# First attention's key roots: four GpSimd powers replaced by eleven VectorE instructions

## The chip, the cores and the metric

The kernel runs on one core of one Trainium2 chip. The metric is the device time of one execution in microseconds (us). One profiled execution gives the trace from which every row below is read; times of single instructions are in that trace's us, counted from the start of its span.

## The reference, cut to what matters

Four sublayers are applied to x of shape 16 x 256 x 128, each between two layer norms with a residual: a phasor convolution, a mixture of 8 experts, a 16-head attention with l2-normed queries and keys, and a second mixture. The part that the change touches is the norm of the keys:

```python
def _l2norm(t):
    return t / jnp.maximum(jnp.linalg.norm(t, axis=-1, keepdims=True), 1e-12)
q = _l2norm(q) * q_scale
k = _l2norm(k) * k_scale
sim = jnp.einsum('bhid,bhjd->bhij', q, k) * ATTN_SCALE
...
attn = jax.nn.softmax(sim, axis=-1)
```

One reciprocal root per token and head is needed for the keys, 128 x 64 numbers for a group of 512 tokens.

## The kernel before, in words

The 16 sequences go through in G = 8 groups of two. A group is 512 tokens, T = 4 tiles of 128, with tokens on the partitions. Up to four groups are under way at once, each in another sublayer. Each engine plays a list of steps in an order written out by hand: `PROLOGUE`, `FIRST`, `MIDDLE` (five times), `LAST_L`, `LAST_A`, `LAST_F`. A name like `a_kss.0.1` is a step and its arguments. In `FIRST` the attention (`a_`) of group 0 runs beside the first mixture (`l_`) of group 1 and the convolution (`e_` for group 2, `E_` for group 1). Engines meet only through semaphores, and each engine takes its list in order, so a step that waits holds up all that stand behind it.

The steps around the change, in group 0:

- ScalarE squares the keys, and TensorE sums the squares by head (`a_kr`) and turns the sums (`a_kt`). VectorE's `a_kss` (`a_ksums`, L1579) clamps the sums and divides by 64, 128x64 in `k_sumsq`.
- GpSimd's `a_kss.b.part` (`k_norms`, L943) raises them to -0.5, in four instructions of 128x16 numbers each, into `rnorm[:, 0]`. In `FIRST` GpSimd's list has them as "a_ss.2 a_kss.0.0 l_turn2 a_ss.3 l_res a_kss.0.1 a_keep a_kss.1.0 a_kss.1.1 e_stats a_scores.0". Here `a_ss.t` (L937) is the same power for the queries of tile t, and `l_turn2`, `l_res`, `e_stats` (L894) are the roots of the layer norms n_y, n_l, n_x.
- ScalarE's `a_scores.c` (L1198 to L1207) takes the exponents of one pair of score tiles with `rnorm[:, 0]` as the scale. It waits for the semaphore `a_kroot`, which counts four in all: step c needs c // 2 + 1. GpSimd's `a_scores.c` then masks (L951) and adds (`late_sum`, L961, which writes the tile mixed), and TensorE's `a_mix.c` uses the mask (L2075) and the sum (L2078).
- VectorE's list in `FIRST` reads "a_kss a_u.2 l_turn2 a_ss.3 l_res a_u.3 l_norm e_stats a_nexp l_turn3 l_route l_pick l_coef l_hg.0 l_hu.0 e_apply l_hg.1". `a_u.t` (L1587) scales the queries of a tile by their roots; `l_turn2` (L1388 to L1393) and `l_res` (L1398 on) are layer norm work, `e_apply` (L1398 too, xn from xin) waits for GpSimd's `e_stats`, and `l_hg.1` (L1528) frees the bank that TensorE's `l_g.2` (L1770) writes. `e_scan` (L1450) is a scan of the convolution.
- TensorE's list has "l_route l_g.0 a_scores.0 l_u.0 l_cT a_nT l_g.1 l_u.1 a_scores.1 l_g.2 a_mix.0 l_c.0 a_scores.2 a_mix.1". The scores are L2028 and L2034; tanh of `l_g.j` on ScalarE is L1127.

Of the kernel before, what the change touches and what calls it, by code (L numbers as in the profile page):

```python
# [20 lines left out]
I32 = mybir.dt.int32  # L21
U32 = mybir.dt.uint32
ALU = mybir.AluOpType
# [52 lines left out]
a_scores.5 a_scores.6 a_scores.7 l_x.0 l_x.1  # L76
""",
    "POOL": """
E_stats a_ss.0 a_ss.1 E_scan a_ss.2 a_kss.0.0 l_turn2 a_ss.3 l_res a_kss.0.1 a_keep a_kss.1.0 a_kss.1.1 e_stats
a_scores.0 a_scores.1 a_scores.2 a_scores.3 e_scan a_scores.4 a_scores.5 a_scores.6 l_dstats.0 a_scores.7 l_dstats.1  # L80
l_astats.0 l_astats.1 a_o.0 a_o.1
""",
# [147 lines left out]
def program(nc, a, out):  # L230
# [4 lines left out]
    T = SEQ * L // P  # L235
    N = T * P
    H, DH, NULLS = 16, 64, 2
# [16 lines left out]
    with ExitStack() as ctx:  # L254
        def sb(name, shape, dt=F32):
            return ctx.enter_context(nc.sbuf_tensor(name, shape, dt))

        def sem(name):
            return ctx.enter_context(nc.semaphore(name))

        def signal(name, per):
            return Signal(sem(name), per)
# [99 lines left out]
        rnorm = sb("rnorm", [P, 2, T, 16])  # L362
# [33 lines left out]
        k_square = [unit[:, i // 2, i % 2, :] for i in range(4)]  # L396
# [168 lines left out]
        a_ss = signal("a_ss", 2 * T)  # L565
# [3 lines left out]
        a_kturn = signal("a_kturn", 1)  # L569
        a_kss = signal("a_kss", 1)  # L570
        a_kroot = signal("a_kroot", 4)
        a_unit = signal("a_unit", T)
        a_s = signal("a_s", H)
        a_odd1 = signal("a_odd1", H // 2)
# [146 lines left out]
        def known(g):  # L721
            return isinstance(g, int)

        def first(g):
            return known(g) and g == 0
# [532 lines left out]
        def _(dve):  # L1258
# [12 lines left out]
            V = nc.vector  # L1271
# [303 lines left out]
            def a_ksums(g):  # L1575
                dve.wait_ge(a_kturn.sem, a_kturn.at(g))
                if not first(g):
                    dve.wait_ge(a_kroot.sem, a_kroot.at(g - 1))
                V.tensor_scalar(k_sumsq.rearrange("p t (c j) -> p t c j", j=4),  # L1579
                                bank[3][:].rearrange("p (t c j) -> p t c j", t=T, j=32)[:, :, :, 0:4],  # L1580
                                1e-24, 1.0 / 64.0, ALU.max, ALU.mult).then_inc(a_kss.sem, 1)

            def a_units(g, t):
                dve.wait_ge(a_root.sem, a_root.at(g, t + 1))
                dve.wait_ge(a_took.sem, a_took.at(g, use("m", t, 1) + 1))
                raw = unit[:, t % 2, 2:4, :].rearrange("p j (h d) -> p (j h) d", d=DH)
                V.tensor_tensor(raw, raw, rnorm[:, 1, t, :].unsqueeze(2).to_broadcast([P, H, DH]), ALU.mult).then_inc(a_unit.sem, 1)  # L1587
# [157 lines left out]
            def f_end(g):  # L1745
# [8 lines left out]
                "l_norm": l_norm, "l_turn3": l_turn3, "l_ct": l_cT, "l_xl": l_xl, "l_route": l_route, "l_pick": l_pick_, "l_coef": l_coef, "l_hg": l_hg_, "l_hu": l_hu_,  # L1754
                "l_hc": l_hc_, "l_dstats": l_down_, "l_end": l_end, "l_astats": a_stats, "l_aapply": a_apply,
                "a_null": a_null, "a_ss": a_sums, "a_kss": a_ksums, "a_u": a_units,
                "a_nexp": a_nexp_, "a_nt": a_nrows_, "a_mix": a_mixes, "a_o": a_out_, "a_end": a_end,
                "f_stats": f_stats, "f_apply": f_apply, "f_turn": f_lows, "f_route": f_route, "f_pick": f_pick_, "f_ce": f_ce_,
# [471 lines left out]
def build(nc, inputs):  # L2230

    arrays, args = {}, {}
    for name, value in inputs.items():
        v = np.ascontiguousarray(value)
        arrays[f"in_{name}"] = v
        args[name] = nc.dram_tensor(f"in_{name}", v.shape, mybir.dt.from_np(v.dtype), kind="ExternalInput").ap()
    out = nc.dram_tensor("out_0", inputs["L0_attn_x"].shape, F32, kind="ExternalOutput").ap()
    program(nc, args, out)
    return arrays
# [10 lines left out]
```

## Time and profile before

| | |
|---|---|
| median of 3 runs | 931.28 us (929.42 to 932.6) |
| the profiled execution's own time | 930.28 us |
| its span | 928.6 us |
| busy share | PE 94%, PEld 75%, DVE 83%, ACT 63%, POOL 61% |
| granted clock of TensorE, mean | 0.997 |

The span is what the trace covers; the execution's own time is 1.68 us more, for what lies around it. PE is TensorE's matmuls, PEld its weight loads, DVE VectorE, ACT ScalarE, POOL GpSimd. A busy share is a mean over the whole span, and says nothing of the one stretch in which the first attention runs.

### The profile page before, as it was taken

How to read it: one execution, taken by the hardware profiler on the slowest of the kernel's cores; microseconds unless marked ns; L12 is line 12 of the kernel's file. 1: busy time of each engine (PE TensorE's matmuls, PEld its weight loads, DVE VectorE, ACT ScalarE, POOL GpSimd, SP SyncE). 2: the span in 40 equal slices, each digit the busy share in tenths (PEclk: the TensorE clock that was granted, in tenths of full speed). 3: DMA queues.
4: the chain of work that ended last, by engine and by line, in shares of the span. 5: the costliest groups of instructions: out<-in, count | busy, mean ns of one | idle time of the engine just before them, and what ended most of it. 6: DMA issues, size and time to landing. Idle time of an engine off the chain costs nothing.

```text
span 928.6 us, 21350 instructions
## 1 busy us (share of the span) xinstructions
PE 874.9 (94%) x8095; PEld 692.8 (75%) x8095; DVE 767.0 (83%) x2457; ACT 586.4 (63%) x1255; POOL 568.4 (61%) x503
## 2 busy tenths in 40 slices
PE   0997899999999999999999999999999999998886
PEld 0675678687877878687777878688787878777666
DVE  6787898789998899889997899879997678865576
ACT  4528773876477672976557672976648683885631
POOL 5118773687557774677547874668635964487623
PEclk9999999999999999999999999999999999999999
DMA  6400000000000000000000000000000000000000
GB/s 161 117 1 0 13 2 1 1 13 1 14 1 1 12 2 13 1 13 2 13 2 1 12 2 14 1 12 2 14 1 1 2 1 14 0 1 1 14 1 12
DMA packets 21991, 11.46 MB, mean 12 GB/s; under 512 B 7552, under 2 KB 21248, under 8 KB 21760
## 3 DMA queue, kind: packets, MB, share of 16 engines
q1 hardware_dynamic: 20032, 9.50, 3.7%
q8 instruction: 64, 1.05, 0.5%
q10 hardware_dynamic: 1856, 0.59, 0.3%
q14 instruction: 39, 0.32, 0.1%
HBM read 7.99 MB, written 2.10 MB: 11 GB/s over the span
## 4 chain that ended last, share of the span: by engine, by line
PE 75%; DVE 8%; POOL 8%; ACT 5%; issue 3%; DMA 0%; DVEq 0%; POOLq 0%; ACTq 0%
PE bank L1770 8%; PE bank L1772 7%; PE bank L1771 7%; PE bank L2100 6%; PE bank L1783 5%; PE bank L1936 4%; PE bank L2028 4%; PE bank L2085 4%; PE bank L2202 3%; PE bank L2208 3%; PE bank L2034 3%; PE bank L2087 2%; PE bank L1992 2%; POOL mixed L961 2%; PE bank L2177 2%
## 5 line engine op out<-in xcount | busy, mean ns | idle before, releaser
L937 POOL TENSOR_TENSOR rnorm<-sumsq,minus_half 128x16 f32<-128x16 f32 x32 | 95.8, 2994 | 57.3 <-DVE sumsq L1573 57.2
L1201 ACT ACTIVATE square<-bank,bias_k,rnorm 128x256 f32<-128x256 f32 x128 | 65.8, 571 | 54.0 <-PE bank L2028 54.0
L2028 PE MATMUL bank<-qT,kT 64*128 64x256 f32 x512 | 96.6, 387 | 0.0
L943 POOL TENSOR_TENSOR rnorm<-unit,minus_half 128x16 f32<-128x16 f32 x32 | 93.3, 2928 | 1.6 <-DVE unit L1579 1.6
L2034 PE MATMUL bank<-qT,kT 64*128 64x128 f32 x512 | 84.0, 284 | 5.5 <-ACT unit L1207 3.9
L2034 PEld LDWEIGHTS bank<-qT,kT 64*128 64x128 f32 x512 | 71.0, 186 | 18.8 <-ACT unit L1207 6.1
L951 POOL TENSOR_SCALAR_AFFINE_SELECT square<-square 128x512 f32<-128x512 f32 x64 | 45.2, 707 | 48.9 <-ACT square L1207 48.7
L1131 ACT ACTIVATE xaT_hi<-bank 128x256 fp32r<-128x256 f32 x16 | 5.9, 384 | 108.5 <-PE bank L1944 108.2
L2028 PEld LDWEIGHTS bank<-qT,kT 64*128 64x128 f32 x512 | 68.8, 186 | 0.2
L951 POOL TENSOR_SCALAR_AFFINE_SELECT unit<-unit 128x512 f32<-128x512 f32 x64 | 41.0, 646 | 40.6 <-ACT unit L1207 40.6
L2100 PE MATMUL bank<-w_out,qT 128*128 128x128 f32 x512 | 62.7, 276 | 1.5 <-DVE qT L1622 1.5
L2100 PEld LDWEIGHTS bank<-w_out,qT 128*128 128x128 f32 x512 | 59.7, 192 | 2.1 <-DVE qT L1622 1.7
L1201 ACT ACTIVATE unit<-bank,bias_k,rnorm 128x256 f32<-128x256 f32 x96 | 51.4, 574 | 15.3 <-PE bank L2028 15.3
L1587 DVE TENSOR_TENSOR unit<-unit,rnorm 128x1024 f32<-128x1024 f32 x32 | 45.7, 1427 | 15.1 <-POOL rnorm L937 15.1
L1207 ACT ACTIVATE unit<-bank,bias_k,rnorm 128x128 f32<-128x128 f32 x128 | 52.7, 478 | 0.0
L1207 ACT ACTIVATE square<-bank,bias_k,rnorm 128x128 f32<-128x128 f32 x128 | 52.4, 473 | 0.0
L1570 DVE TENSOR_REDUCE sumsq<-square 128x16 f32<-128x1024 f32 x32 | 38.9, 1215 | 13.2 <-ACT square L1147 13.2
L1783 PEld LDWEIGHTS bank<-ident,unit 128*128 128x128 f32 x296 | 33.7, 141 | 20.1 <-DVE unit L1587 10.5
L1167 ACT ACTIVATE qT<-bank,qk_scale 128x512 f32<-128x512 f32 x64 | 40.5, 689 | 11.5 <-PE bank L1783 11.5
L1140 ACT ACTIVATE unit<-bank 128x512 f32<-128x512 f32 x64 | 36.8, 600 | 16.0 <-PE bank L1772 15.0
L1622 DVE TENSOR_TENSOR qT<-bank,mixed 128x512 f32<-128x512 f32 x64 | 44.2, 691 | 2.2
L1783 PE MATMUL bank<-ident,unit 128*128 128x128 f32 x296 | 39.7, 275 | 6.6 <-DVE unit L1587 3.6
(419 smaller groups left out, 2910.3 us busy)
## 6 DMA issues: line engine op xcount, KB each, us to landing
xin<-in_L_attn_x SPq DMA_DIRECT2D x7, 256.0 KB, 2.8
out<-x SPq DMA_DIRECT2D x7, 256.0 KB, 2.3
square<-in_L_attn_w_kv SPq DMA_DIRECT2D x1, 1024.0 KB, 6.3
unit<-in_L_attn_w_q SPq DMA_DIRECT2D x1, 512.0 KB, 5.6
w_out<-in_L_attn_w_out SPq DMA_DIRECT2D x8, 64.0 KB, 2.1
xin<-in_L_attn_x ACTq DMA_DIRECT2D x1, 256.0 KB, 3.1
unit<-in_L_ffn_experts_gate ACTq DMA_DIRECT2D x1, 256.0 KB, 3.4
unit<-in_L_ffn_experts_up SPq DMA_DIRECT2D x1, 256.0 KB, 2.9
```

The lines of the kernel that those rows point to most:

```text
L937: pool.tensor_tensor(rnorm[:, 1, t, :], sumsq[:, t % 2, :], minus_half[:], ALU.pow).then_inc(a_root.sem, 1)
L943: pool.tensor_tensor(rnorm[:, 0, ts, hs], k_sumsq[:, ts, hs], minus_half[:, hs].unsqueeze(1).to_broadcast([P, 2, H // 2]), ALU.pow).then_i ...
L951: pool.affine_select(out=pd, in_=pd, compare_op=ALU.is_ge, fill=0.0, base=0, pattern=[[0, 4], [1, P]], channel_multiplier=-1).then_inc(a_m ...
L1201: last = act.activation(early(pr, j), k0, ACT.Exp, bias=bias_k0[:, h:h + 1], scale=by)
L1207: last = act.activation(late(pr, j), bank[2][:, 2 * P * s + P * j:2 * P * s + P * (j + 1)], ACT.Exp, bias=bias_k1[:, h:h + 1], scale=by)
L1770: mm(dst, left.hi, right.hi, start=True, stop=False)
L1771: mm(dst, left.hi, right.lo, start=False, stop=False)
L1772: return mm(dst, left.lo, right.hi, start=False, stop=True)
L1783: last = nc.tensor.transpose(dst[:, t * P:(t + 1) * P], src(t), ident[:])
L2028: return mm(bank[s][:, 2 * P * i:2 * P * (i + 1)], kT[rs, p, 2 * P * b:2 * P * b + P], qT[rs, p, 2 * P * b:2 * P * (b + 1)], start=True, s ...
L2034: return mm(bank[2][:, 2 * P * s + P * i:2 * P * s + P * (i + 1)], kT[rs, p, ts], qT[rs, p, ts], start=True, stop=True)
L2100: mm(out_bank(g, h)[:, ts], outT[:, c, ts], w_out[:, c, :], start=(c == 0), stop=False)
```

## The change

The four `a_kss` steps are gone from GpSimd's list in `FIRST`; the lists of the other stages keep theirs. VectorE, right behind the clamp of `a_kss` and only in group 0, runs a new function `k_roots`. It shifts the bits of the number right by one, takes them from a constant, and improves the guess by three Newton steps of three instructions: 11 instructions over 128x64 numbers, each waiting for the one before it through the new semaphore `k_newton`. The last raises `a_kroot` by four.

```diff
-E_stats a_ss.0 a_ss.1 E_scan a_ss.2 a_kss.0.0 l_turn2 a_ss.3 l_res a_kss.0.1 a_keep a_kss.1.0 a_kss.1.1 e_stats
+E_stats a_ss.0 a_ss.1 E_scan a_ss.2 l_turn2 a_ss.3 l_res a_keep e_stats
...
+        k_newton = sem("k_newton")
...
                                 1e-24, 1.0 / 64.0, ALU.max, ALU.mult).then_inc(a_kss.sem, 1)
+                if first(g):
+                    k_roots()
+
+            def k_roots():
+
+                ss = k_square[1][:, 0:T * H]
+                tmp = k_square[1][:, T * H:2 * T * H]
+                y = rnorm[:, 0, :, :].rearrange("p t h -> p (t h)")
+                dve.wait_ge(a_kss.sem, a_kss.at(0))
+                V.tensor_scalar(tmp.bitcast(I32), ss.bitcast(I32), 1, None, ALU.logical_shift_right).then_inc(k_newton, 1)
+                dve.wait_ge(k_newton, 1)
+                V.tensor_scalar(y.bitcast(I32), tmp.bitcast(I32), -1.0, float(0x5f3759df), ALU.mult, ALU.add).then_inc(k_newton, 1)
+                for k in range(3):
+                    dve.wait_ge(k_newton, 3 * k + 2)
+                    V.scalar_tensor_tensor(out=tmp, in0=y, scalar=-0.5, in1=y, op0=ALU.mult, op1=ALU.mult).then_inc(k_newton, 1)
+                    dve.wait_ge(k_newton, 3 * k + 3)
+                    V.tensor_tensor(tmp, tmp, ss, ALU.mult).then_inc(k_newton, 1)
+                    dve.wait_ge(k_newton, 3 * k + 4)
+                    done = V.scalar_tensor_tensor(out=y, in0=tmp, scalar=1.5, in1=y, op0=ALU.add, op1=ALU.mult)
+                    if k < 2:
+                        done.then_inc(k_newton, 1)
+                    else:
+                        done.then_inc(a_kroot.sem, 4)
```

## Rows read from the trace of the kernel before

**Rows 1.** The page: busy time, share of the span and instructions of each engine.
```profile
PE 874.9 (94%) x8095; PEld 692.8 (75%) x8095; DVE 767.0 (83%) x2457; ACT 586.4 (63%) x1255; POOL 568.4 (61%) x503
```

**Rows 2.** Busy time of each engine in two stretches (us; count in brackets).
```profile
85.00:110.00 25.00, 18.61 (x118) 14.45 (x116) 19.88 (x75) 19.73 (x44) 22.68 (x13) 1.00 0.04 11
110.00:135.00 25.00, 24.84 (x356) 18.30 (x355) 23.97 (x48) 18.03 (x44) 15.72 (x17) 1.00 0.01 3
```

**Rows 3.** The chain that ended last: start us, us, what.
```profile
99.54 5.72 POOL rnorm L943 x2
```

**Rows 4.** Timeline of POOL: start us, us, what [idle before <-releaser].
```profile
85.56 3.81 POOL L943 TENSOR_TENSOR rnorm<-unit,minus_half 128x16 f32<-128x16 f32 x1 [1.61 <-DVE unit L1579]
89.34 1.00 POOL L894 TENSOR_TENSOR n_y_rstd<-n_y_var,minus_half 128x4 f32<-128x4 f32 x1
90.32 2.89 POOL L937 TENSOR_TENSOR rnorm<-sumsq,minus_half 128x16 f32<-128x16 f32 x1
94.08 1.92 POOL L894 TENSOR_TENSOR n_l_rstd<-n_l_var,minus_half 128x4 f32<-128x4 f32 x1 [0.87 <-DVE n_l_var L1393]
...
106.20 1.22 POOL L951 TENSOR_SCALAR_AFFINE_SELECT unit<-unit 128x512 f32<-128x512 f32 x2
...
111.91 1.27 POOL L961 TENSOR_TENSOR mixed<-square 128x512 f32<-128x512 f32 x1
...
118.11 1.27 POOL L961 TENSOR_TENSOR mixed<-unit 128x512 f32<-128x512 f32 x1
```

**Rows 5.** Timeline of DVE, 85 to 106 us.
```profile
85.26 0.23 DVE L1579 TENSOR_SCALAR unit<-bank 128x64 f32<-128x64 f32 x1 [2.71 <-PE bank L1783]
85.40 1.22 DVE L1587 TENSOR_TENSOR unit<-unit,rnorm 128x1024 f32<-128x1024 f32 x1
87.09 0.89 DVE L1388 BATCH_NORM_STATS2 n_y_six<-bank 128x6 f32<-128x128 f32 x4 [0.48 <-PE bank L1783]
...
88.51 1.22 DVE L1570 TENSOR_REDUCE sumsq<-square 128x16 f32<-128x1024 f32 x1
89.77 0.18 DVE L1573 TENSOR_SCALAR sumsq<-sumsq 128x16 f32<-128x16 f32 x1
90.38 1.37 DVE L1398 TENSOR_SCALAR xn<-bank,n_y_mv,n_y_rstd 128x128 f32<-128x128 f32 x4 [0.44 <-POOL n_y_rstd L894]
```

**Rows 6.** Timeline of DVE, 106 to 122 us.
```profile
106.27 2.84 DVE L1398 TENSOR_SCALAR xn<-xin,n_x_mv,n_x_rstd 128x128 f32<-128x128 f32 x4 [1.15 <-POOL n_x_rstd L894]
...
111.95 0.17 DVE L1613 TENSOR_TENSOR den<-bank,null_sum 128x8 f32<-128x8 f32 x1
112.15 0.20 DVE L1617 RECIPROCAL recip<-den 128x8 f32<-128x8 f32 x1
...
118.48 3.10 DVE L1450 TENSOR_TENSOR_SCAN conv<-decay_row,conv 128x512 f32<-128x512 f32 x2
```

**Rows 7.** Single lines of DVE: count, duration in ns min/median/max, first and last start.
```profile
L1627 DVE TENSOR_TENSOR mixed<-mixed,recip x16: 214/215/651, 127.3 to 884.8; 128x64 f32<-128x64 f32 x16
L1593 DVE SCALAR_TENSOR_TENSOR null_s<-null_s,bias_null x8: 291/1128/1133, 98.8 to 829.3; 128x128 f32<-128x128 f32 x8
L1398 DVE TENSOR_SCALAR xn<-x,n_l_mv,n_l_rstd x4: 343/344/346, 96.0 to 96.8; 128x128 f32<-128x128 f32 x4
```

**Rows 8.** Timeline of PE.
```profile
91.16 0.63 PE L1783 MATMUL bank<-ident,unit 128*128 128x128 f32 x4 [2.28 <-ACT val L1174]
...
106.62 0.37 PE L2034 MATMUL bank<-qT,kT 64*128 64x128 f32 x1 [0.35 <-ACT unit L1207]
...
109.77 0.50 PE L1770 MATMUL bank<-xlT_hi,w_gate_hi 128*128 128x512 f32 x1 [1.57 <-DVE unit L1528]
...
112.55 0.60 PE L2034 MATMUL bank<-qT,kT 64*128 64x128 f32 x3
...
114.52 0.40 PE L2078 MATMUL bank<-mixed,ones 128*32 128x128 f32 x8
```

**Rows 9.** Timeline of ACT.
```profile
110.29 0.83 ACT L1207 ACTIVATE square<-bank,bias_k,rnorm 128x128 f32<-128x128 f32 x2
```

## The prediction

> **What bounds the kernel now.** I read the page first. TensorE is busy for 94% of the span [rows 1], so in most places only a change of its work or of its few waits moves the end. The stretches say that the first attention is one of the other places: from 85 to 110 us TensorE works 18.61 of 25 us, and GpSimd, with 22.68, is the busiest engine; from 110 to 135 us TensorE works 24.84 of 25 again and VectorE 23.97 [rows 2]. So whatever the change brings has to be read from the first stretch, and what counts is how much earlier or later TensorE comes out of it.
>
> The chain in order of time seems to settle the matter: it runs through GpSimd's key roots, 5.72 us of them at 99.54 [rows 3], right up to the root of n_x for which `e_apply` waits. GpSimd's timeline gives the four pieces as 3.81 at 85.56, one of some 2.9 behind the root of n_l (94.08 to 96.00), and 5.72 [rows 3, 4]. But the chain goes back along an engine that is always busy. The waits are what other engines pay for it, and they are small: VectorE waits 0.44 us for the root of n_y before `l_res` (90.38), and 1.15 us for n_x before `e_apply` (106.27) [rows 5, 6]. TensorE's own wait is 1.57 us at `l_g.2`, for VectorE's `l_hg.1`, which stands right behind `e_apply` [rows 8]. That is the place where GpSimd's lateness reaches TensorE.
>
> **What is removed.** Four powers go, 3.81 + 2.9 + 5.72 = 12.4 us of GpSimd. The scores' exponents don't wait for them (the first piece is there at 89.4, and ScalarE reaches `a_scores.0` only behind 100 us). What comes sooner is what stood behind: the root of n_y, which could start when VectorE has its variance (about 88.7, not 89.34), and the root of n_x, ready some 4 us before VectorE gets to `e_apply`. VectorE's steps before `e_apply` end at about 105.1, so it would save the 1.15 us of waiting, and `e_apply` itself, 2.84 us beside GpSimd's masks, where four tensor_scalars of this shape at 0.34 us each take 1.4 at most [rows 6, 7].
>
> **What is added.** Eleven instructions over 128x64 numbers on VectorE, each waiting for the last. No row shows the two on integers, nor such a chain. The nearest in width is L1627, two SBUF inputs, 128x64, 0.215 us at the median; a tensor_scalar of 128x64 from PSUM takes 0.23 [rows 7, 5]. The gap to the next one that waits for it: a 0.17 us instruction at 111.95 is followed at 112.15, so 0.03 to 0.04 [rows 6]. I take 0.215 + 0.04 = 0.255 a step, p, and 11 p = 2.8 us. Bounds: from below the narrowest dependent one, 0.17 + 0.04 = 0.21, giving 2.3; from above a tensor_scalar twice as wide, 0.343 + 0.04 = 0.38, giving 4.2 [rows 7].
>
> A rule speaks here, and against many small instructions. The 11 steps cost nearly as much as wide ones would: 8 numbers a partition take 0.17 us, 64 take 0.215 [rows 6, 7]. The Trainium skill (VectorE: DVE Perf Modes, section on the TRN2 errata) says that an SBUF instruction pays a fixed extra cost, with a table entry of 58 cycles plus the width at 0.96 GHz. By that table a step would be 0.13 us, 11 of them 1.4 us without gaps, and the change would come to 1.4 - 2.4 = -1.0 us by the sum below; the same section says that the table is too low for single instructions, and the rows agree with that.
>
> **What stands behind the Newton steps.** `a_u.2`, `l_turn2`, `a_ss.3`, `l_res`, in order. The clamp starts at 85.26 and ends at 85.49; the next one that waits for it starts at 85.53. The chain ends at 85.53 + 2.8 = 88.3. Independent instructions start 0.09 before the end of the last (85.40 against 85.49), so `a_u.2` starts at 88.2 instead of 85.40. Before, VectorE then had 0.48 us of waiting for TensorE (87.09) and the 0.44 us above; now both are gone and all is back to back. By the starts in rows 5: `a_u.2` 1.22 - 0.09 = 1.13; the statistics of `l_turn2` 88.51 - 87.09 = 1.42; the sum of `a_ss.3` 89.77 - 88.51 = 1.26; its clamp 0.18 - 0.09 = 0.09; together 3.90. `l_res` starts at 88.2 + 3.9 = 92.1 instead of 90.38. I call this delay S: S = 11 p - 1.1 = 1.7 us. GpSimd is idle by then; the root of n_y is out 3.8 us behind the start of `a_u.2`, just in time, and is not the last to come.
>
> What of the work between is hidden: TensorE's `a_t.2` needs `a_u.2`, now at 89.5 rather than 88.3, but its second half waits until 91.16 for ScalarE to free a bank anyway [rows 8]. From `l_res` on VectorE, TensorE and ScalarE wait for one another (root of n_l, `l_turn3`, `l_route`, the scores), with no slack that I can find, so all of it comes S later up to `a_scores.1` on TensorE at 106.62 + 1.7.
>
> **What is given back.** Behind `a_scores.1`, TensorE had 1.57 us of waiting at 109.77 [rows 8]. `e_apply` no longer waits and is over long before ScalarE's tanh, so `l_hg.1` comes in time and `l_g.2` starts S - 1.57 = 0.15 us later than before. The pair of scores that ScalarE takes next ends at 111.12 + S (110.29 + 0.83) [rows 9], and frees a bank for `a_scores.2`, which started at 112.55: it has 1.37 us of slack [rows 8], 0.06 less the hand-over. GpSimd's add of that pair ends at 113.18 + S (111.91 + 1.27) [rows 4], and TensorE's `a_mix.1` wanted it at 114.52, so with 0.05 for the hand-over there were 1.29 us of slack [rows 8]. The last one binds: TensorE goes on S - 1.3 = 0.4 us later. Behind it TensorE is full [rows 2], and nothing later is tied to a fixed time, so 0.4 us stay to the end.
>
> In one line: change = 11 p - 1.1 - 1.3 = 11 p - 2.4. If the Newton steps cost nothing, `l_turn2` would still wait for TensorE until 87.09 and S would be -0.5, the change -1.8 us: this is all that GpSimd's 12.4 us are worth. With p = 0.21 it is -0.1, with 0.255 +0.4, with 0.38 +1.8. On the profiled execution's 930.28 us the likeliest is 930.7. The median of the runs shown is 1.0 above that execution; on it, 931.28 + 0.4 = 931.7. Its own range is 931.2 to 933.1, before the scatter of the runs, which is 3.2 us wide over three. A difference under 0.3%, 2.8 us, is about what a measurement of this kernel can't tell from none.
>
> **The rivals.**
>
> The chain is right (5%). If GpSimd's pieces lay on the path in full, 12.4 - 2.8 = 9.6 us would go: 921.7. For it speaks only the chain [rows 3]; against it the waits of 0.44 and 1.15 us, and that the pair of 5.72 us holds back nothing but the root of n_x and the masks.
>
> The Newton steps are dear (8%). Each is a wait on VectorE's own semaphore, and two of them are on integers. L1593, a two-input instruction like six of these, takes 1.13 us at the median where it falls beside GpSimd's powers, and 0.29 where it doesn't [rows 7]. GpSimd is idle from 84 to 91 us in the new order, so I don't expect it. From p = 0.47 on the change is over +2.8 us, and at 0.6 it is +4.2: 935.5.
>
> The engines collide elsewhere (12%). `e_apply` took 2.84 us beside masks from 106.20, and the two scans 3.10 us at 118.48 beside an add at 118.11 to 119.38 [rows 4, 6]. In the new order the first is at about 106.8 to 108, beside only one mask. Should the add and the scan part as well, up to 1.27 us of blocking comes back, and the change is 0.4 - 1.3 = -0.9: 930.4. Should they collide anew, it is +1.7: 933. Both are within 0.3%. The Trainium skill (SBUF — State Buffer, section Who interferes with whom) has it that a VectorE instruction with two SBUF inputs and a GpSimd one that reads SBUF exclude each other, and that the second to issue stands until the first is done. The trace agrees where it can be seen: 2.84 against 1.4 us.
>
> The change does nothing measurable for other reasons, my sum being off by a slack that I missed on either side: that is inside the forecast.
>
> **How the numbers follow.** My sum (within 0.3%) has 75%, the collisions 12%, both no difference; the chain 5%, dear steps 8%. The rest of the doubt is the scatter, which can push either side over the bound. Faster by over 0.3%: 0.09; within: 0.81; slower: 0.10. The range goes from the collisions' gain less scatter, 929.0, to the upper bound of p (933.1) with scatter, 934.2; outside stay the chain and dear steps, and a little scatter.
>
> **What would show it.** In the new profile: GpSimd idle from 84 to some 91 us; eleven instructions of 128x64 from 85.5 to 88.3 on VectorE; `a_u.2` at 88.2; `l_res` at 92.1 with no wait for the root of n_y; `a_scores.1` on TensorE at 108.3; no wait of TensorE for L1528 at `l_g.2`, which starts at about 109.9; `e_apply` with no wait and under 2 us; TensorE's L2078 of `a_mix.1` at 114.9. I am wrong if the steps take more than 0.38 us each, if something between 92 and 106 us had slack that takes S up, or if a stretch behind 115 us gives back or adds more than a microsecond.

## The result, and the profile after

| | before | changed |
|---|---|---|
| median | 930.07 us (20 runs, 929.42 to 932.72) | 932.60 us (20 runs, 932.17 to 934.20) |
| profiled execution's own time | 930.28 us | 932.91 us |
| span | 928.6 us | 931.2 us |

The ratio is 1.0027, interval 1.0021 to 1.0034: the changed kernel is 2.5 us slower. That is just inside the 0.3% that I called no difference, and with twenty runs of each it is a difference all the same. I forecast +0.4 us.

Timeline of VectorE in the changed kernel, 85 to 109 us (start us, us, line, operation). These are the rows that answer to [rows 5]:

```profile
85.55 0.23 DVE L1580 TENSOR_SCALAR unit<-bank 128x64 f32<-128x64 f32 x1 [2.70 <-PE bank L1807]
85.81 0.20 DVE L1592 TENSOR_SCALAR unit<-unit 128x64 int32<-128x64 int32 x1
86.04 0.20 DVE L1594 TENSOR_SCALAR rnorm<-unit 128x64 int32<-128x64 int32 x1
86.27 0.23 DVE L1597 SCALAR_TENSOR_TENSOR unit<-rnorm 128x64 f32<-128x64 f32 x1
...
88.42 0.23 DVE L1601 SCALAR_TENSOR_TENSOR rnorm<-unit,rnorm 128x64 f32<-128x64 f32 x1
88.56 1.22 DVE L1611 TENSOR_TENSOR unit<-unit,rnorm 128x1024 f32<-128x1024 f32 x1
...
92.45 1.36 DVE L1399 TENSOR_SCALAR xn<-bank,n_y_mv,n_y_rstd 128x128 f32<-128x128 f32 x4
...
98.09 1.38 DVE L1399 TENSOR_SCALAR xn<-x,n_l_mv,n_l_rstd 128x128 f32<-128x128 f32 x4 [0.90 <-POOL n_l_rstd L895]
...
102.49 0.69 DVE L1477 TENSOR_TENSOR xlT_lo<-bank,xlT_hi 128x512 fp32r<-128x512 f32 x1 [1.10 <-ACT xlT_hi L1112]
...
108.54 1.24 DVE L1399 TENSOR_SCALAR xn<-xin,n_x_mv,n_x_rstd 128x128 f32<-128x128 f32 x4
```

This execution is 0.29 us later than the one before already at 34 us and again at 84.6 us, ahead of the change, so that much has to be taken off. The eleven steps then take 85.81 to 88.65, 2.84 us; `l_res` starts at 92.45 and no longer waits for a root; `e_apply` (108.54) doesn't wait either and is down from 2.84 to 1.24 us. But at 102.49 VectorE waits for ScalarE, which it didn't before. TensorE, which was to be S later and no more, shows why. The eight transposes of `a_t.3` before:

```profile
95.19 1.09 PE L1783 MATMUL bank<-ident,unit 128*128 128x128 f32 x8 [1.98 <-DVE unit L1587]
```

TensorE's timeline in the changed kernel:

```profile
91.46 0.63 PE L1807 MATMUL bank<-ident,unit 128*128 128x128 f32 x4 [0.96 <-ACT val L1175]
...
97.25 1.82 PE L1807 MATMUL bank<-ident,unit 128*128 128x128 f32 x8 [3.74 <-DVE unit L1611]
98.72 0.78 PE L1794 MATMUL bank<-w_kv_hi,xaT_hi 128*128 128x512 f32 x1
99.29 0.63 PE L1795 MATMUL bank<-w_kv_lo,xaT_hi 128*128 128x512 f32 x1
...
101.84 0.39 PE L1795 MATMUL bank<-w_kv_lo,xaT_hi 128*128 128x512 f32 x1
```

And the busy time by stretch (PE, PEld, DVE, ACT, POOL, then the granted clock):

```profile
85.00:97.00 12.00, 6.46 (x34) 4.70 (x33) 10.76 (x39) 7.70 (x15) 4.77 (x3) 1.00 0.07 22
97.00:101.00 4.00, 3.75 (x14) 3.33 (x15) 3.03 (x15) 1.97 (x3) 1.67 (x3) 0.57 0.02 4
101.00:105.00 4.00, 3.93 (x23) 2.85 (x21) 1.65 (x9) 2.28 (x4) 0.96 (x1) 1.00 0.00 0
```

TensorE stood idle for 3.74 us ahead of `a_t.3`, where it had waited 1.98 us before. From 97.4 us its granted clock is half, 1.2 of 2.4 GHz, for 3.4 us. The same matmul takes 0.63 us at 99.29 and 0.39 us at 101.84, and eight transposes take 1.82 us where they took 1.09.

To see where each run gains or loses, I took the start of the n-th matmul of TensorE less that of the same matmul in the kernel before, at points named by their time there. The last column but one is the stage by itself: the shift at 140 us less that at 84.6.

| run | 84.6 | 95.2 | 101.5 | 109.8 | 119 | 140 | stage | end |
|---|---|---|---|---|---|---|---|---|
| changed | +0.29 | +2.06 | +3.51 | +1.87 | +2.27 | +2.17 | +1.87 | +2.63 |
| x1_warm | +0.16 | +1.94 | +2.20 | +0.56 | +0.96 | +0.86 | +0.69 | +1.30 |
| x2_two_steps | +0.45 | +1.44 | +2.71 | +1.07 | +1.46 | +1.35 | +0.89 | +1.79 |
| x3_order | -0.06 | -0.05 | +1.63 | -0.01 | +0.39 | +0.32 | +0.38 | +0.32 |
| x4_add_only | +1.92 | +3.62 | +4.95 | +3.31 | +3.70 | +3.60 | +1.68 | +3.61 |
| x5_fill | +1.32 | +3.09 | +3.36 | +1.71 | +2.10 | +1.98 | +0.66 | +2.17 |
| x6_behind | -0.09 | -0.63 | +1.52 | -0.13 | +0.27 | +0.21 | +0.30 | +0.63 |
| x7_split | +0.38 | -0.15 | +0.37 | -1.09 | -0.72 | -0.82 | -1.21 | -0.88 |
| x8_one_step | +0.47 | +0.68 | +0.93 | -0.71 | -0.31 | -0.41 | -0.88 | +0.04 |
| x9_split_keep | -0.16 | -0.70 | -0.57 | -1.74 | -1.34 | -1.45 | -1.29 | -1.33 |
| x10_split_fill | -0.38 | -0.92 | -0.79 | -1.97 | -1.58 | -1.66 | -1.28 | -1.81 |
| x11_before_fill | -0.30 | -0.30 | -0.30 | -0.30 | -0.29 | -0.28 | +0.02 | -0.31 |
| x12_seed | +0.17 | -0.37 | -0.10 | -1.74 | -1.34 | -1.45 | -1.63 | -1.42 |

In the changed kernel S is 2.06 - 0.29 = 1.77 us at `a_t.3`; it jumps by 1.45 up to 101.5, and 1.64 comes back at `l_g.2`. The first column differs from run to run, ahead of any difference between the kernels, so a single execution can't be compared at its end; the stage column can. What the first column follows is the clock: matmuls of 128x512 that take 0.63 us at first take 0.39 us from about 31.9 us on in the kernel before, from 32.6 in the changed kernel (+0.29) and from 33.1 in x8 (+0.47), and in x4 and x5 (+1.92, +1.32) the clock was at half once more from 50.8 to 54.2 us.

### The profile page after: what moved, and what is told of

Its sections match the earlier page's. It is cut to its first block, busy times and chain, and to the rows that moved or that the text cites. A ratio compares the mean times of both kernels' runs of the same rounds, so it can differ in the third digit from the quotient of the medians.

```text
span 931.2 us, 21358 instructions
## 1 busy us (share of the span) xinstructions
PE 877.2 (94%) x8095; PEld 694.1 (75%) x8095; DVE 765.5 (82%) x2468; ACT 586.8 (63%) x1255; POOL 556.9 (60%) x499
## 4 chain that ended last, share of the span: by engine, by line
PE 74%; DVE 9%; POOL 7%; ACT 6%; issue 3%; DMA 0%; DVEq 0%; ACTq 0%; POOLq 0%
PE bank L1794 8%; PE bank L1796 7%; PE bank L1795 7%; PE bank L2124 6%; PE bank L1807 5%; PE bank L1960 4%; PE bank L2052 4%; PE bank L2109 4%; PE bank L2226 3%; PE bank L2232 3%; PE bank L2058 3%; POOL mixed L962 2%; PE bank L2111 2%; PE bank L2016 2%; PE bank L2201 2%
## 5 line engine op out<-in xcount | busy, mean ns | idle before, releaser
L944 POOL TENSOR_TENSOR rnorm<-unit,minus_half 128x16 f32<-128x16 f32 x28 | 81.0, 2905 | 0.0
```

What stands on the lines that cost most here:

```text
L944: pool.tensor_tensor(rnorm[:, 0, ts, hs], k_sumsq[:, ts, hs], minus_half[:, hs].unsqueeze(1).to_broadcast([P, 2, H // 2]), ALU.pow).then_i ...
```

## The experiments

Two theories. **Cold clock:** the delay by itself is worth what my sum says, and the rest is TensorE's pause, which lowers its clock. **Missed slack:** each us that VectorE is late reaches the end, and the clock has no part in it.

**x1_warm.** Dummy matmuls ahead of `a_t.3`:

```diff
             def a_t(g, t):
+                if first(g) and t == 3:
+                    for _ in range(8):
+                        mm(bank[4][:], w_kv.hi[:, 0:P], w_kv.hi[:, 0:N], start=True, stop=True)
```

> The changed kernel with eight matmuls of 128x512 (1.9 us) whose result nothing reads, on TensorE right ahead of a_t.3, where it stands idle for 3.74 us in the changed kernel. The cold-clock theory (the pause lowers the granted clock to 0.5 for 3.4 us, and this costs some 1.5 of the 2.5 us): no stretch of lowered clock between 90 and 105 us, time 1.5 us under the changed kernel, +1.0 us against the kernel before (ratio about 1.001). The missed-slack theory (every us that VectorE is later reaches the end, whatever the clock): time as the changed kernel, +2.5 us (1.0027).

Measured: median 933.20 us (6 runs), ratio 1.0030 (1.0018 to 1.0042). By the median, no help. But the profiled execution, at 931.58 the fastest of the six, is the one with the clock up. Its TensorE and its stretches:

```profile
97.13 1.09 PE L1807 MATMUL bank<-ident,unit 128*128 128x128 f32 x8 [1.92 <-DVE unit L1611]
97.98 0.48 PE L1794 MATMUL bank<-w_kv_hi,xaT_hi 128*128 128x512 f32 x1
```

```profile
97.00:101.00 4.00, 3.87 (x23) 3.29 (x24) 3.00 (x16) 3.04 (x6) 1.67 (x3) 1.00 0.00 0
```

The stage costs 0.69 us here and 1.87 us in the changed kernel, with the same delay at `a_t.3` (1.78 and 1.77): the clock is 1.2 us. The other five runs, at 933.03 to 933.85, had a mean clock of 0.992 to 0.994 against 0.996. They have no trace, so that the clock fell in this stage there is likely and not shown. x5 fills all three pauses.

**x2_two_steps.** `for k in range(2)` in `k_roots`, the roots less exact.

> The changed kernel with two Newton steps instead of three: 8 instructions instead of 11, the roots less exact. VectorE is 0.78 us earlier, and TensorE's pause ahead of a_t.3 is 2.96 us instead of 3.74. The cold-clock theory: if the clock stays up over the shorter pause, 0.8 + 1.5 = 2.3 us under the changed kernel, +0.2 us against the kernel before (1.000); if it falls all the same, +1.7 us (1.0018). The missed-slack theory: +1.7 us with the clock at 1.00.

Measured: median 931.93 us, ratio 1.0017 (1.0008 to 1.0026). TensorE's pause was 2.98 us, and the clock fell:

```profile
96.63 1.09 PE L1807 MATMUL bank<-ident,unit 128*128 128x128 f32 x8 [2.98 <-DVE unit L1611]
```

```profile
97.70:101.00 3.30, 3.30 (x12) 2.62 (x11) 2.97 (x15) 2.09 (x4) 0.97 (x2) 0.50 0.00 0
```

The stage is 0.98 us under the changed kernel's, of which 0.78 are three instructions of 0.26. The time fits both theories; only the clock, which missed slack wants at 1.00, is against that one: it was 0.50.

**x3_order.** The kernel before, with GpSimd's list changed and a wait that keeps `l_hg.1` from overwriting the sums:

```diff
-... l_res a_kss.0.1 a_keep a_kss.1.0 a_kss.1.1 e_stats
+... l_res a_kss.0.1 a_keep e_stats a_kss.1.0 a_kss.1.1
...
                 dve.wait_ge(l_tanh.sem, l_tanh.at(g, j + 1))
+                if known(g) and g == 1 and j == 1:
+                    dve.wait_ge(a_kroot.sem, a_kroot.at(0))
```

> The kernel before (roots on GpSimd) with e_stats moved up in GpSimd's list, ahead of the last two key pieces, and l_hg.1 waiting for these. My sum says that GpSimd's pieces cost TensorE its wait of 1.57 us at l_g.2 alone, of which the next slacks let 1.3 us through: -1.3 us against the kernel before (0.9986). If the collisions of masks and VectorE take it back: 0. If the chain of waits were right (12 us on the path): the same 12 us stay and nothing is gained either.

Measured: median 929.90 us, ratio 0.9997 (0.9988 to 1.0006): inconclusive. In the profiled execution the clock fell here too, and for longer:

```profile
92.00:99.00 7.00, 5.70 (x18) 4.30 (x18) 5.89 (x26) 3.74 (x7) 6.13 (x4) 0.52 0.13 40
```

The shift goes from -0.05 to +1.63 over that stretch, and the stage is +0.38; less the 1.7 of that jump it would be -1.3, as I reckoned. That is worked out from one execution, and not shown by the times.

**x4_add_only.** The changed kernel with GpSimd's list of before, and `y` in `k_roots` a scratch tile:

```diff
-                y = rnorm[:, 0, :, :].rearrange("p t h -> p (t h)")
+                y = k_square[1][:, 2 * T * H:3 * T * H]
```

> The changed kernel with GpSimd's four key pieces put back: the Newton steps write to a scratch tile that nothing reads. Delay S = 1.7 us plus 1.5 us of lowered clock and none of the 1.8 us that the removal is worth in my sum, less what GpSimd's list hides: +4.0 us against the kernel before (1.0043). Rival, that the removal is worth nothing: as the changed kernel, +2.5 us (1.0027).

Measured: median 932.25 us, ratio 1.0020 (1.0010 to 1.0029). The +4.0 expected is out of the interval, and the rival holds: with the Newton steps in front, taking GpSimd's 12.4 us away is worth nothing. The stage is +1.68 against +1.87. GpSimd's timeline shows that the delay itself had made the room:

```profile
103.13 5.76 POOL L944 TENSOR_TENSOR rnorm<-unit,minus_half 128x16 f32<-128x16 f32 x2
108.85 1.01 POOL L895 TENSOR_TENSOR n_x_rstd<-n_x_var,minus_half 128x4 f32<-128x4 f32 x1
109.83 0.64 POOL L952 TENSOR_SCALAR_AFFINE_SELECT unit<-unit 128x512 f32<-128x512 f32 x1
```

`e_apply` gets its root at 109.86, just as VectorE is through with what stands ahead of it, and `l_hg.1` behind it waits 0.72 us for ScalarE's tanh in any case.

**x5_fill.** Dummy matmuls in all three pauses:

```diff
+                    if first(g) and t >= 2 and (t, k) != (3, 1):
+                        for _ in range({(2, 0): 4, (2, 1): 3, (3, 0): 14}[t, k]):
+                            mm(bank[4][:], w_kv.hi[:, 0:P], w_kv.hi[:, 0:N], start=True, stop=True)
```

> The changed kernel with dummy matmuls of 128x512 in all three of TensorE's pauses between 88 and 97 us: 4 ahead of the first half of a_t.2, 3 ahead of its second half, 14 ahead of a_t.3, so that TensorE hardly stands idle; their result is read by nothing. In the profiled run of x1_warm the clock stayed up and the stage came out 1.2 us earlier than in the changed kernel, but five of its six runs took 1.5 us more than the profiled one. The cold-clock theory: with the pauses full the clock stays up in nearly all runs, +1.2 us against the kernel before (1.0013). The missed-slack theory: +2.5 us (1.0027).

Measured: median 931.50 us, ratio 1.0010 (1.0001 to 1.0019), where 1.0013 was expected. All eleven runs have a mean clock of 0.995 to 0.997; the changed kernel's twenty have 0.992 to 0.995. That alone would prove little, as the 35 runs of the kernel before that were measured beside x5 have 0.992 to 0.997: a mean doesn't say where the clock fell. TensorE's waits and clock:

```profile
90.87 0.66 PE L1807 MATMUL bank<-ident,unit 128*128 128x128 f32 x4 [0.17 <-DVE unit L1611]
92.49 0.63 PE L1807 MATMUL bank<-ident,unit 128*128 128x128 f32 x4 [0.27 <-ACT val L1175]
...
98.28 1.09 PE L1807 MATMUL bank<-ident,unit 128*128 128x128 f32 x8 [0.53 <-DVE unit L1611]
```

```profile
97.00:101.00 4.00, 3.47 (x23) 2.60 (x21) 3.10 (x9) 1.96 (x4) 2.49 (x2) 1.00 0.19 56
```

The delay at `a_t.3` is still 3.09 - 1.32 = 1.77 us, and the stage costs 0.66 us. So VectorE was exactly as late as in the changed kernel, and 1.2 us of the loss are gone: missed slack falls, and its 1.0027 lies outside the interval. (The profiled execution, 932.47, was the slowest of its eleven: it was 1.3 us late ahead of the stage, for the lowered clock at 51 us.)

**x6_behind.** `k_roots` called at the end of `a_units` for t = 3 instead of in `a_ksums`:

```diff
-                if first(g):
-                    k_roots()
...
                 V.tensor_tensor(raw, raw, rnorm[:, 1, t, :].unsqueeze(2).to_broadcast([P, H, DH]), ALU.mult).then_inc(a_unit.sem, 1)
+                if first(g) and t == 3:
+                    k_roots()
```

> The changed kernel with the eleven Newton instructions behind a_u.3 instead of behind a_kss. VectorE then waits for the root of n_l in their shadow (0.9 us), and TensorE's pause ahead of a_t.3 shrinks from 3.7 to about 1.4 us, with another of 1.6 us ahead of l_turn3. The cold-clock theory: delay at l_norm S = +1.4 us, clock at 1.00 through the stage, +0.1 to +0.6 us against the kernel before (1.0004). The missed-slack theory, by which the work added to VectorE is what counts: +2.0 us or more (1.002).

Measured: median 931.12 us, ratio 1.0006 (0.9997 to 1.0015). The pauses are as I reckoned:

```profile
94.56 1.09 PE L1807 MATMUL bank<-ident,unit 128*128 128x128 f32 x8 [1.43 <-DVE unit L1609]
98.72 0.66 PE L1807 MATMUL bank<-ident,xn 128*128 128x128 f32 x4 [1.67 <-DVE xn L1399]
```

The stage is +0.30. Each against its own runs of the kernel before, the same eleven instructions cost +0.6 us here (not clear of zero) and +2.5 us behind `a_kss`, 1.9 us less; in the stage it is 1.6 us less, and missed slack wanted +2.0 or more.

**x7_split.** The guess and first step behind `a_u.3`, the other two behind `l_turn3`:

```diff
-                for k in range(3):
+                for k in ((0,), (1, 2))[part]:
...
+                if first(g) and t == 3:
+                    k_roots(0)
...
                 low(xlT, bank[3][:])
+                if known(g) and g == 1:
+                    k_roots(1)
```

> The Newton steps in two parts: the guess and the first step (5 instructions, 1.3 us) behind a_u.3, where VectorE waited 0.9 us for the root of n_l, the other two steps (6 instructions, 1.56 us) behind l_turn3, where it waited 1.15 us for TensorE. Cold-clock theory with my sum: S = -0.5 + 0.4 + 0.4 = +0.3 us, change S - 1.3 = -1.0 us against the kernel before (0.999). Missed-slack theory: +1 us or more.

Measured: median 929.66 us, ratio 0.9993 (0.9984 to 1.0002); the stage is -1.21 us, where -1.0 was expected. The ratio excludes missed slack's +1 us, and doesn't exclude zero. VectorE's second part sits where it waited for TensorE before:

```profile
99.96 0.22 DVE L1598 SCALAR_TENSOR_TENSOR unit<-rnorm 128x64 f32<-128x64 f32 x1
...
101.32 0.23 DVE L1602 SCALAR_TENSOR_TENSOR rnorm<-unit,rnorm 128x64 f32<-128x64 f32 x1
101.46 0.22 DVE L1497 TENSOR_REDUCE logit<-bank 128x32 f32<-128x64 f32 x1
```

**x8_one_step.** `for k in range(1)`, the roots good to some 0.2%.

> The changed kernel with one Newton step instead of three: 5 instructions, roots good to some 0.2% only. VectorE is 1.56 us earlier than in the changed kernel, TensorE's pause ahead of a_t.3 is 2.2 us. My sum: 5 x 0.26 - 2.4 = -1.1 us against the kernel before with the clock up (0.9988); with the clock lowered all the same about +0.1 (1.000). Missed-slack theory: +2.5 - 1.6 = +0.9 us (1.001).

Measured: median 930.33 us, ratio 1.0003 (0.9994 to 1.0011). The stage is -0.88 us with the clock up over a pause of 2.20 us. By the end it is +0.04: 0.45 us were lost behind the stage, 0.37 of them between 366 and 370 us. What took them I didn't follow up. The median lies between the theories (-1.1 and +0.9) and decides nothing.

**x9_split_keep.** x7 with "l_res e_stats a_keep" in GpSimd's list.

> x7_split with GpSimd's copy a_keep behind e_stats instead of ahead of it, so that it no longer runs beside VectorE's l_norm. In x7 and in the changed kernel the four instructions of l_norm took 1.38 us, in the kernel before 1.11. If the copy is what they collide with: l_norm back to 1.11 us, the stage 0.2 us better than x7's -1.2: -1.1 us in the median against the kernel before (0.9988). If not: as x7, 0.9991, and l_norm at 1.38 us.

Measured: median 929.52 us, ratio 0.9992 (0.9983 to 1.0001), stage -1.29: as x7. The premise was wrong: the four of `l_norm` were at 0.33 us each in x7 already (0.34 here), since the copy no longer fell on them. It fell on the last instruction of the Newton steps' first part instead, and x9 moved it away from there. GpSimd's copy and that instruction in x7, then the instruction in x9:

```profile
95.81 0.61 POOL L934 COPY x<-x2n 128x512 f32<-128x512 f32 x1
95.88 0.62 DVE L1602 SCALAR_TENSOR_TENSOR rnorm<-unit,rnorm 128x64 f32<-128x64 f32 x1
95.33 0.23 DVE L1602 SCALAR_TENSOR_TENSOR rnorm<-unit,rnorm 128x64 f32<-128x64 f32 x1
```

So it is the copy. In the changed kernel it starts at 98.02, and the first of `l_norm`'s four, at 98.09, takes 0.61 us where the other three take 0.33; x1, x2, x5, x8 and x12 have the same. In x4, with the same Newton steps and the copy at 102.44, all four take 0.34.

**x10_split_fill.** x9 with 8 dummy matmuls ahead of the second half of `a_t.2` and 5 ahead of `a_t.3`, written as in x5.

> x9_split_keep with dummy matmuls of 128x512 in TensorE's two pauses of the stage: 8 ahead of the second half of a_t.2, 5 ahead of a_t.3; their result is read by nothing. If the pauses of 2.3 and 1.4 us still lower the clock in some runs: fewer slow runs, median some 0.3 us under x9, 0.9985. If these pauses don't matter: as x9.

Measured: median 929.02 us, ratio 0.9986 (0.9977 to 0.9995). The only version with all three Newton steps that is faster than the kernel before beyond its interval. That it is better than x9 (0.9992) isn't shown: each ratio lies in the other's interval.

**x11_before_fill.** The kernel before with 8 and 7 dummy matmuls in the same places.

> The kernel before with dummy matmuls in the same two pauses (8 ahead of the second half of a_t.2, 7 ahead of a_t.3, where it stood idle for 2.28 and 1.98 us), results read by nothing. In x3_order, with pauses as in the kernel before, the profiled run had the clock lowered from 92 to 99 us, so some runs of the kernel before may pay too: the median falls by up to 0.4 us (0.9996). If the kernel before never pays here: 1.000.

Measured: median 930.27 us, ratio 0.9999 (0.9990 to 1.0008), stage +0.02. The dummies cost nothing, and bring nothing where the pauses are 2.28 and 1.98 us. So dummies don't speed up a kernel by themselves, and what x5 won it won where the clock had fallen.

**x12_seed.** The first two instructions of `k_roots` alone, the second raising `a_kroot` by four, and the dummies of x11. The roots are off by up to some 3%.

> The changed kernel with the first two of the eleven instructions alone (the guess from the bits, good to some 3%, no Newton step), and dummy matmuls in TensorE's pauses as in x11_before_fill. This is the removal of GpSimd's 12.4 us with next to nothing in their place. My sum puts the removal at -1.8 us, S at -0.5 us, with all behind it as it was; two instructions of 0.26 us eat some 0.0 to 0.1 of it, as VectorE had 0.5 us to wait there: stage -1.7 us, median 0.9981. If the chain of waits were right: -12 us (0.987).

Measured: median 928.84 us, ratio 0.9981 (0.9972 to 0.9989), stage -1.63. This is what GpSimd's 12.4 us are worth when next to nothing takes their place (x11 has the dummies at +0.02): TensorE is busy for 23.73 of the 25 us from 85 on, eight and seven dummies counted, against 18.61 [rows 2].

```profile
85.00:110.00 25.00, 23.73 (x168) 18.42 (x170) 20.44 (x80) 19.86 (x44) 10.48 (x9) 1.00 0.04 12
```

## Why the prediction was right and where it was wrong

**Right: the chain of waits isn't the path.** 12.4 us of GpSimd removed are worth 1.7 us (x12: stage -1.63, ratio 0.9981), where I had -1.8 and the chain says -12.

**Right: the price of the steps.** 11 instructions took 2.84 us against 2.8; those on integers took 0.20 us, the others 0.23. VectorE was S = 1.77 us late at `a_t.3` against 1.7.

**Right: what is given back.** 1.64 us came back at `l_g.2` (3.51 to 1.87) against 1.57; then 0.4 were lost again by 119, as the add on GpSimd's side binds: it ends at 116.70, and `a_mix.1` uses it at 116.75, where before it had ended at 113.18 for 114.52 [rows 4, 8].

```profile
115.42 1.28 POOL L962 TENSOR_TENSOR mixed<-square 128x512 f32<-128x512 f32 x1
116.75 0.43 PE L2102 MATMUL bank<-mixed,ones 128*32 128x128 f32 x8
```

With the clock up the stage is +0.69 and +0.66 (x1, x5) against my +0.4. The rest is `l_norm`, on which the copy now fell: 1.38 us instead of the 1.12 of before, so that in x1 and x5 S grew from 1.77 to 2.04 by 101.5.

```profile
96.03 1.12 DVE L1398 TENSOR_SCALAR xn<-x,n_l_mv,n_l_rstd 128x128 f32<-128x128 f32 x4 [0.90 <-POOL n_l_rstd L894]
```

**Wrong: "with no slack that I can find, so all of it comes S later up to `a_scores.1`".** This step has no term for TensorE's clock. I had 2.28 and 1.98 us of idle time of TensorE in the trace, and knew that an S of 1.7 makes the second one 3.7; I never asked what the pause does to the clock. It fell to 0.5 for 3.4 us and cost 1.87 - 0.69 = 1.2 us in the stage (0.66 in x5 gives the same). This is the largest missing term of +2.5 against +0.4. The signs that I had named came in up to there and failed behind it: with 0.29 taken off, `l_res` started at 92.16 against 92.1, but `a_scores.1` at 109.84 against 108.3.

**Luck.** 932.60 us lies in my range of 929.0 to 934.2, and 1 us from my likeliest 931.7, but not by my mechanism. The change was six times the forecast one; the upper part of the range, in which it lies, stood for steps of up to 0.38 us and for scatter, and the steps took 0.26. And 1.2 us of the closeness are the start that I added to, 931.28 from three runs, where twenty runs give 930.07.

**Wrong: where L1593 is slow.** For the rival of dear steps I wrote that it takes 1.13 us beside GpSimd's powers and 0.29 where it isn't beside them. The trace of before has it the other way round: at 726.70 it takes 0.29 us in the middle of a power, and at 199.16, beside a product of 128x512 (`weigh_biases`, L982), 1.13.

```profile
199.10 1.05 POOL L982 TENSOR_TENSOR ce_rows<-row_out,pick 128x512 f32<-128x512 f32 x1 [1.32 <-DVE xn L1398]
199.16 1.13 DVE L1593 SCALAR_TENSOR_TENSOR null_s<-null_s,bias_null 128x128 f32<-128x128 f32 x1
725.28 2.90 POOL L943 TENSOR_TENSOR rnorm<-unit,minus_half 128x16 f32<-128x16 f32 x1
726.70 0.29 DVE L1593 SCALAR_TENSOR_TENSOR null_s<-null_s,bias_null 128x128 f32<-128x128 f32 x1
```

So powers were no reason to fear for the Newton steps; a wide product or copy was, as x7 shows for the copy. I also took `e_apply` (2.84 against 1.4 us) for an instance of two SBUF inputs. It is a tensor_scalar with one; the case with two is that of x7, 0.62 against 0.23 us.

**A small term behind the stage.** From 717 to 729 us the changed kernel loses another 0.37 us. At one instruction VectorE waits for nothing that the profile shows:

```profile
719.83 1.22 DVE L1571 TENSOR_REDUCE sumsq<-square 128x16 f32<-128x1024 f32 x1 [0.26 <-issue]
```

x1, x5 and x6 have the same stall at the same instruction, x2 has one at the next but one, and all four lose 0.35 to 0.37 us there. The kernel before doesn't have it, and neither do the others, x4 among them, which has the same eleven instructions at the same place. Added up for the two profiled executions: 0.29 ahead of the stage, 0.69 for the delay, 1.18 for the clock, 0.46 behind it, in all 2.62 of the 2.63 us. The 0.29 is scatter, of the clock at 32 us; 0.37 of the 0.46 come again in the profiles of four other versions and so belong to the kernel. Why the stall falls where it does stays open.

**The rivals.** The chain: refuted by x12. Dear steps: refuted by the trace, at 0.26 us each; though the time came out near that rival's bound, it was not by its mechanism. Collisions elsewhere: one came, +0.26 us at `l_norm`, and the scans at `e_scan` took 3.04 us as against 3.10, so nothing came back there. That the removal is worth nothing, which I had not listed apart, is true of this version (x4) and false by itself (x12): the two halves of the change are not a sum. Late VectorE work hides what the early end of GpSimd would bring.

## What to carry to other kernels

Before work is moved onto an engine, find the place in that engine's list where it waits anyway: the same eleven instructions cost 2.5 us behind `a_kss` and 0.6 behind `a_u.3`, and cut in two at VectorE's two waits they came out at -0.7, inside the noise of zero (-1.2 in the stage). Look too at what the other engine does at the new place: GpSimd's copy of 0.61 us held the instruction of the Newton steps (x7) or of `l_norm` (the changed kernel) that started 0.07 us behind it. When a delay lengthens a pause of TensorE, ask for a second price, that of the clock behind the pause; matmuls into a free bank that fill all the pauses about the place took most of it away (x5), and cost nothing where the clock had stayed up (x11); filling one in part did not by the median (x1). And judge an engine's removal by the waits that others have for it, 0.44 and 1.15 us here, not by its share of the chain.

## What the runs showed of the hardware that I had not expected

The granted clock fell to half for 3.4 us behind pauses of 3.74 us (changed kernel) and 2.98 (x2) and at the end of one of 3.69 (x4), and stayed up behind 2.28 and 1.98 us in the profiled run of the kernel before, 2.20 in x8 and 1.92 in x1. But the length of the pause doesn't settle it. In x3 the clock fell at 92.2 us, 1.1 us behind a pause of 2.28 us, and stayed down for about 7 us. In x3, x4 and x5 it fell at 51 us, in the other eleven traces it didn't, though all these kernels have TensorE do the same work there. And in every trace but x3's, that of the kernel before too, it was at half for 3.4 us from a point between 62 and 64.5 us on, where TensorE had not waited longer than 0.78 us since 36 us. x5, then the kernel before at the same place, then the kernel before at 63 us:

```profile
50.80:54.10 3.30, 3.30 (x16) 3.30 (x17) 3.15 (x2) 0.60 (x2) 0.00 (x0) 0.50 0.00 0
50.80:54.10 3.30, 3.08 (x27) 3.11 (x28) 3.15 (x3) 0.90 (x2) 0.00 (x0) 1.00 0.00 0
62.70:66.00 3.30, 3.30 (x9) 2.60 (x8) 2.86 (x12) 0.38 (x1) 0.00 (x0) 0.50 0.01 2
```

The Trainium skill (TensorE: Matmul & The Clock Gate, section What's actually happening) says that half the clock is the array's default and its state once it has been idle, and that what watches its activity doesn't start anew with the kernel, so that the moment at which the clock rises varies from run to run. The traces agree with both as far as they go: half behind the pause of 3.74 us, and a rise at 31.9 us before, 32.6 in the changed kernel, 33.1 in x8 and 30.3 in x5, in the same matmuls. Why the clock falls at 51 and 63 us, with hardly a pause ahead, no run here shows. What is shown is narrower: with the changed kernel's delay, filling the pauses kept the clock up in this stage (x5), and that was worth 1.2 us.
